# Pairwise field projection on one core: the next x by a gather on GpSimd without eight partitions, and its transpose eight steps later

## What is computed

```
xi = x[:, pi, :]                              # 2048 x 496 x 64
xj = x[:, pj, :]
proj = einsum('bpd,pod->bpo', xi, W)          # each row of xi by its pair's matrix
return proj * xj                              # 2048 x 496 x 64, 260 MB
```

## Time and profile before

| | |
|---|---|
| median of three runs | 684.69 us |
| the profiled execution | 684.55 us |
| its span | 682.7 us |
| PE busy | 573.4 us (84%) |
| DVE busy | 409.3 us (60%) |
| POOL busy | 391.9 us (57%) |
| ACT busy | 208.4 us (31%) |
| bytes moved by DMA | 285.20 MB, 418 GB/s over the span |
| of the chain that ended last: matmuls (line 294) | 47% |
| of it: DMA x_sb<-x_dram | 37% |

### The profile page before, as it was taken

How to read it: one execution, slowest core, us unless ns; L and a number is a source line. 1 busy time by engine, 2 the same in 40 slices (tenths; PEclk the granted TensorE clock), 3 DMA queues, 4 the chain that set the end, 5 groups by cost and what they waited for, 6 DMA issues and landing times.

```text
span 682.7 us, 7003 instructions
## 1 busy us (share of the span) xinstructions
PE 573.4 (84%) x2704; PEld 363.3 (53%) x2704; DVE 409.3 (60%) x528; ACT 208.4 (31%) x257; POOL 391.9 (57%) x228
## 2 busy tenths in 40 slices
PE   6899989979799796988969889697996979979930
PEld 4565646546465564645646456464654646546520
DVE  1677775837567473764837638386583756837730
ACT  3334333323233333332323323233332323332300
POOL 1768674646566374674646836468464665647720
PEclk9999999989899898998989989899898989989975
DMA  8999999999999999999999999999999999999995
GB/s 336 386 426 425 439 438 423 434 436 428 432 432 431 432 428 436 435 427 428 431 427 429 428 404 410 428 421 407 426 426 424 422 415 429 399 439 419 421 421 233
DMA packets 15648, 285.20 MB, mean 418 GB/s; under 512 B 1744, under 2 KB 1872, under 8 KB 3856
## 3 DMA queue, kind: packets, MB, share of 16 engines
q1 hardware_dynamic: 13472, 270.28, 93.3%
q10 hardware_dynamic: 2160, 14.75, 5.1%
HBM read 24.97 MB, written 260.05 MB: 417 GB/s over the span
## 4 chain that ended last, share of the span: by engine, by line
PE 55%; DMA 37%; DVE 2%; SPq 1%; issue 1%; ACT 0%; DVEq 0%; ACTq 0%
PE proj L294 47%; DMA x_sb<-x_dram 37%; PE proj L272 7%; DVE staged L338 2%; SPq L199 1%; ACT staged L260 0%; SPq L203 0%; SPq L197 0%; SPq L196 0%; SPq L195 0%; DVEq L133 0%; ACTq L259 0%
## 5 line engine op out<-in xcount | busy, mean ns | idle before, releaser
L338 DVE TENSOR_TENSOR staged<-proj,x_sb 128x1024 f32<-128x1024 f32 (+7 forms) x528 | 409.3, 826 | 246.5 <-PE proj L294 210.8
L221 POOL TENSOR_TENSOR staged<-staged,x_sb 128x1024 f32<-128x1024 f32 (+4 forms) x224 | 391.7, 1755 | 261.4 <-ACT staged L260 258.4
L294 PE MATMUL proj<-w_sb,x_t 64*128 64x512 f32 (+7 forms) x2432 | 518.7, 533 | 3.6 <-DVE staged L338 2.1
L294 PEld LDWEIGHTS proj<-w_sb,x_t 64*128 64x128 f32 x2432 | 313.1, 188 | 204.3 <-issue 121.6
L260 ACT ACTIVATE staged<-proj 128x1024 f32<-128x1024 f32 (+4 forms) x224 | 174.6, 787 | 356.5 <-PE proj L294 329.1
L272 PE MATMUL proj<-ident_sb,x_sb 128*128 128x128 f32 x256 | 52.6, 390 | 71.2 <-DMA x_sb<-x_dram 71.2
L272 PEld LDWEIGHTS proj<-ident_sb,x_sb 128*128 128x128 f32 x256 | 47.1, 208 | 80.3 <-DMA x_sb<-x_dram 79.8
L236 ACT ACTIVATE x_t<-proj 128x1024 f32<-128x1024 f32 x32 | 32.5, 1024 | 86.2 <-PE proj L272 86.1
L311 PE MATMUL proj<-ident_sb 128*128 128x128 f32 x16 | 3.4, 405 | 5.6 <-DMA ident_sb<-ident_dram 5.6
L311 PEld LDWEIGHTS proj<-ident_sb 128*128 128x128 f32 x16 | 3.2, 223 | 5.6 <-DMA ident_sb<-ident_dram 5.6
L236 ACT ACT_TABLE_LOAD x1 | 1.3, 1283 | 1.2 <-PEq L368 1.2
## 6 DMA issues: line engine op xcount, KB each, us to landing
out_dram<-staged SPq DMA_DIRECT2D x14, 4896.0 KB, 26.0
out_dram<-staged SPq DMA_DIRECT2D x14, 3936.0 KB, 23.0
out_dram<-staged SPq DMA_DIRECT2D x14, 3776.0 KB, 27.7
out_dram<-staged SPq DMA_DIRECT2D x14, 3264.0 KB, 27.7
x_sb<-x_dram ACTq DMA_DIRECT2D x14, 1024.0 KB, 17.8
out_dram<-staged SPq DMA_DIRECT2D x2, 1952.0 KB, 16.8
out_dram<-staged SPq DMA_DIRECT2D x2, 1824.0 KB, 20.6
out_dram<-staged SPq DMA_DIRECT2D x2, 1728.0 KB, 21.8
```

Source lines behind the costliest of these rows:

```text
L221: last = nc.gpsimd.tensor_tensor(product, product, x_sb[tile.parity][:, j * dim:(j + n) * dim], ALU.mult)
L294: last = nc.tensor.matmul(proj[b][h][:, at:at + width], x_t[tile.parity][half, i // 2, :], w_sb[half, col:col + width], start=True, stop=True)
L338: last = nc.vector.tensor_tensor(staged_part(item, i, j, n), proj[b][h][:, at:at + n * dim], x_sb[tile.parity][:, j * dim:(j + n) * dim], ...
```

## The change

Three things change. The turn moves from before step 10 to before step 18, on PE and on ACT. The next x is fetched by POOL instead of ACT, before POOL's step 4: an indirect DMA that takes for partition p the row of x named in `rows_sb[p, tile]`. For partitions 28 to 35 that table holds a number beyond x, and the bounds check leaves them out. These eight partitions (64 KB) are loaded by ACT with a plain DMA, where it loaded all of x before. POOL waits for that small load before it issues the gather; PE waits for both at the turn. The table of row numbers (128 x 16 numbers, 8 KB) is loaded once by SP ahead of the first store, and the second tile's x gets a semaphore of its own.

```diff
-TURN_BEFORE = 10
+TURN_BEFORE = 18
 LOAD_BEFORE = 3
+GATHER_BEFORE = 4
...
+SKIPPED = range(28, 36)
+NO_ROW = 1 << 20
...
-            sp.dma_start(x_sb[1][:], x[P:2 * P, :]).then_inc(x_loaded[1], 16)
+            sp.dma_start(x_sb[1][:], x[P:2 * P, :]).then_inc(x_second_loaded, 16)
+            sp.dma_start(rows_sb[:], rows).then_inc(rows_loaded, 16)
...
         @block.gpsimd
         def _(pool):
+            def load_x(tile):
+
+                _, b, use = list(items(Tile(tile.number - 1, 1 - tile.parity, None)))[-1]
+
+                pool.wait_ge(emptied[b][1], use + 1)
+                pool.wait_ge(pool_scaled[group_of[pool_steps[-1]]], tile.number)
+                to = tile.number + 1
+
+                pool.wait_ge(x_rest_loaded[1 - tile.parity], 16 * (to // 2))
+                nc.gpsimd.indirect_dma_start(
+                    x_sb[1 - tile.parity][:], None, x,
+                    bass.IndirectOffsetOnAxis(ap=rows_sb[:, to:to + 1], axis=0),
+                    bounds_check=batch - 1, oob_is_err=False).then_inc(x_loaded[1 - tile.parity], 16)
+
             def emit(tile):
                 for item, b, use in items(tile):
+                    if item == GATHER_BEFORE and not tile.first and not tile.last:
+                        if tile.number == 1:
+                            pool.wait_ge(rows_loaded, 16)
+                        load_x(tile)
...
-                act.dma_start(x_sb[1 - tile.parity][:], x[bass.ds((tile.number + 1) * P, P), :]
-                              ).then_inc(x_loaded[1 - tile.parity], 16)
+                row = (tile.number + 1) * P
+                act.dma_start(x_sb[1 - tile.parity][SKIPPED.start:SKIPPED.stop, :],
+                              x[row + SKIPPED.start:row + SKIPPED.stop, :]
+                              ).then_inc(x_rest_loaded[1 - tile.parity], 16)
...
                     if item == "turn":
-                        pe.wait_ge(x_loaded[1 - tile.parity], 16 * tile.half + 16)
+
+                        if tile.first:
+                            pe.wait_ge(x_second_loaded, 16)
+                        else:
+                            loads = tile.half + 1 if tile.parity else tile.half
+                            pe.wait_ge(x_loaded[1 - tile.parity], 16 * loads)
+                            pe.wait_ge(x_rest_loaded[1 - tile.parity], 16 * loads)
...
+    rows = np.arange(batch, dtype=np.uint32).reshape(-1, P).T.copy()
+    rows[SKIPPED.start:SKIPPED.stop] = NO_ROW
```

More of the change, by code:

```diff
@@ L6 @@
 F32 = mybir.dt.float32
+U32 = mybir.dt.uint32
 ALU = mybir.AluOpType
@@ L71, in __init__, with field_pair_project @@
         self.first = isinstance(number, int) and number == 0
-def field_pair_project(nc, x, w, ident, out, fields, dim):
+def field_pair_project(nc, x, w, ident, rows, out, fields, dim):
     batch = x.shape[0]
@@ L145, in field_pair_project @@
         ident_sb = sb("ident_sb", [P, P])
+        rows_sb = sb("rows_sb", [P, tiles], U32)
         staged = [sb(f"staged{k}", [P, n * dim]) for k, (_, n) in enumerate(slot_range)]
@@ L151, in field_pair_project @@
         ident_loaded = sem("ident_loaded")
+        rows_loaded = sem("rows_loaded")
         x_first_loaded = [sem(f"x_first_loaded{h}") for h in range(2)]
+        x_second_loaded = sem("x_second_loaded")
         x_loaded = [sem(f"x_loaded{h}") for h in range(2)]
+        x_rest_loaded = [sem(f"x_rest_loaded{h}") for h in range(2)]
         w_loaded = [sem(f"w_loaded{c}") for c in range(len(w_cuts) - 1)]
@@ L237, in turned_out, with load_skipped @@
                         "p k b -> p (k b)"), proj[b][h][:], ACT.Copy).then_inc(emptied[b][h], 1)
-            def load_x(tile):
+            def load_skipped(tile):
                 _, b, use = list(items(Tile(tile.number - 1, 1 - tile.parity, None)))[-1]
@@ L250, in emit @@
                     if item == LOAD_BEFORE and not tile.first and not tile.last:
-                        load_x(tile)
+                        load_skipped(tile)
                     if item == "turn":
@@ L366 @@
         "ident_dram": np.eye(P, dtype=np.float32),
+        "rows_dram": rows,
     }
@@ L369 @@
                    dynamic_dma_scratch_size=DMA_SCRATCH)
-    aps = [nc.dram_tensor(n, a.shape, F32, kind="ExternalInput").ap() for n, a in arrays.items()]
+    aps = [nc.dram_tensor(n, a.shape, U32 if a.dtype == np.uint32 else F32, kind="ExternalInput").ap()
+           for n, a in arrays.items()]
     out = nc.dram_tensor("out_dram", (batch, pairs * dim), F32, kind="ExternalOutput").ap()
```

## The result

The changed kernel took 689.92 us (689.72 to 690.12, 4 runs), the kernel before 684.64 us; the ratio is 1.0077, 95% interval 1.0065 to 1.0090. It is slower by 5.3 us. The forecast was 673.5 us; the time lies above the range.

What follows compares the result with a forecast made beforehand. One of 16 DMA engines, slower by 1.02 us a tile, was the bound; its relieved end at 669.5, plus 2.85 after it, 1 for gathered rows and 0.3 for the table, made 673.6, stated as 673.5 us; range 668 to 686 us.

Steps and rivals of the forecast that it cites:

- The reading of the bound: DMA engines: one of 16 is slower by 1.02 us a tile and binds; PE's 5.1 us wait for x is slack.
- The turn alone: Turn before step 18 on PE and ACT: removes the 5.1 us wait for x, but alone is worth 0.
- The gather at GpSimd: Gather on POOL: its issue costs 1.5 us, POOL stays at 31 us a tile, under 40, so cost 0.
- GpSimd's wait for the small load: POOL before the gather: 5 us for ACT's 64 KB load, covered by POOL's spare time, cost 0.
- rival C: POOL becomes the bound if the small load takes 17.8 us: 42.6 us a tile, 706 us; chance 0.04.
- The extra microsecond for gathered rows: Gathered rows may cost more than plain ones, 0 to 10 us in all; 1 us added to the forecast.
- the central term: Eight partitions less in the gather: slow engine at 5 rows, 0.91 us a tile less, 12.7 us in 14 gathers.
- rival B: Slow engine gets a ninth row from ACT's small load: +4.2 us, 688.8 us; with dearer gathered rows, together 0.14.
- the forecast's own split: Rows of x per engine: two engines lose four each, and ACT's eight rows go to eight engines, one each.
- The size of the forecast's own case: Slow engine at five rows, engines with nine ending about the same, near 669.5 us: 673.5 us; chance 0.60.

Runs made afterwards that it cites:

- run 1: The kernel before with only the turn moved from before step 10 to before step 18: 684.63 us, ratio 0.9998.
- run 2: The changed kernel with no partition left out of the gather and no small load by ACT: 684.65 us, ratio 0.9998.
- run 10: The changed kernel with only partitions 16 to 19 left out, loaded by a plain GpSimd DMA before its step 3, none by ACT: 684.81 us, ratio 1.0000.
- run 5: The changed kernel with only partitions 16 to 19 left out of the gather and loaded by ACT: 679.31 us, ratio 0.9921.
- run 6: The changed kernel with only partitions 12 to 15 left out of the gather and loaded by ACT: 684.79 us, ratio 1.0001.
- run 9: The changed kernel with partitions 16 to 19 and 48 to 51 left out, loaded by ACT in two four-row DMAs: 684.05 us, ratio 0.9994.
- run 4: The changed kernel with partitions 12 to 19 left out in place of 28 to 35: 678.82 us, ratio 0.9904.
- run 11: As run 10, but with GpSimd's four-row load before step 1 instead of step 3: 678.96 us, ratio 0.9912.
- run 12: As run 5, but with partitions 16 to 19 left out and loaded by ACT only in every other tile: 678.42 us, ratio 0.9910.
- run 3: The changed kernel with partitions 4 to 11 left out in place of 28 to 35: 689.08 us, ratio 1.0062.
- run 8: The changed kernel with partitions 28 to 35 loaded by ACT in two DMAs of four rows instead of one of eight: 685.6 us, ratio 1.0026.
- run 7: As run 4, but with the turn back before step 10: 789.64 us, ratio 1.153.

## Why the prediction was wrong

**What held.** The reading of the bound: one of 16 DMA engines slower than the rest, PE's wait for x being slack (run 1: the wait gone, 684.63 us). The turn alone at 0 (run 1). The gather at GpSimd at 0 (run 2: 684.65 us; 1.04 us of issue where I took 1.5). GpSimd's wait for the small load, covered: it isn't the bound, rival C didn't come, though such a load takes about 8 us (8.22 us in run 10) where I took 5. The extra microsecond for gathered rows wasn't needed.

**The step that failed** is the central term, "If the slow engine is among those that lose rows". I took 8 - 4 + 1 = 5 rows of x for it. It serves partitions 16 to 19 (runs 5 and 6) and 48 to 51 (the packets of run 9), loses none of 28 to 35 and gets one of ACT's eight: 9 rows, as its packets show. The split itself, two engines with five rows and six with nine, was right; the slow engine stood on its wrong side. Nine rows on it is rival B, which I priced at 688.8 us and gave, with its like, 0.14. Nothing in the trace had spoken for 28 to 35; I let a case that the profile could not tell from others carry 0.60, when two engines of 16 lose rows and eight get one. Counted by engines alone, on the forecast's own split, 2 in 16 are relieved, 6 in 16 get a ninth row and 8 in 16 keep eight; that count was open to me and gives B more than the forecast.

**The size of B.** 4.2 us were forecast for it, 5.3 measured, or 0.38 us a row (5.28 / 14) in place of 0.303; in the whole tiles it is 41.40 - 41.08 = 0.32. Rows added to other engines come out dearer, about 0.5 us (run 9).

**The size of the forecast's own case.** Run 4 is that case: the slow engine has five rows, six engines have nine. It took 678.8 us, not 673.5. So the forecast would have been some 5 us too low even with the slow engine where I put it. The engines left at the end are about as many as have nine rows of x (six in run 4, four in runs 5 and 11), which speaks for added rows that cost more than the 0.303 us of the sum, by which nine-row engines were to need 40.35 us a tile. It isn't shown: run 12 halved the added rows and gained nothing clear. Where the rest goes is open; the runs add the row always with a small DMA of its own, and nothing was tried that adds the one without the other.

**Whose rows.** By the runs alone: leaving out 16 to 19 helps, 12 to 15, 4 to 11 and 28 to 35 don't; an eight-row load by ACT puts a row on the slow engine, a four-row one doesn't. The Trainium skill (DMA: Bandwidth & Descriptors, The descriptor swizzle) puts 16 to 19 on engine 4, 12 to 15 on 3, 28 to 31 on 7 and 32 to 35 on 0. Together with the same page's rule (Why a DMA increments its semaphore by 16 and not by 1) by which an eight-row transfer from ACT uses the eight lowest engines and a four-row one the four lowest, a slow engine 4 gives nine rows in the changed kernel and in run 3 (689.9 and 689.1 us), eight in runs 6 and 8 (684.8 and 685.6), five in run 4 (678.8) and four in run 5 (679.3). More rows go with more time, down to eight; five and four can't be told apart. The packets give the same counts, so the runs agree with both. They don't agree with the remark of the same page of the Trainium skill (Latency and other measured facts) that engines 7 and 15 are usually the slow ones; by its map it is engine 4 here, which the forecast had nothing to tell from the others.

## What to carry to other kernels

A transfer over 128 partitions lands when the slowest DMA engine's rows have; look behind all computing for a stretch in which the share is one sixteenth, and find out whose partitions they are (leave out four at a time) before rebalancing. Skipping the right four partitions in a gather gave 0.9% here, the wrong eight cost 0.8% with the same code. A small load that takes over the skipped rows adds rows to the same few engines each time, so count rows for every engine, the slow one too; and a wait of 5 us a tile on the chain may be worth nothing while another resource is full.

## What was not expected of the hardware

- One engine in 16 needs 41.07 us for what the others do in about 40.05 (an estimate from 432 GB/s), with a kernel that loads and stores the same bytes on all: its store packets of 26 and 31 KB take some 33 ns more each. It was the engine of partitions 16 to 19 on three chips: run 4 ran on one, run 9 on another, runs 5 and 11 on a third.
- One row of 8 KB more per tile on each of four engines, which move 40 rows of 8 to 39 KB in that time, cost nearly the whole gain: 684.05 us with ten rows of x on them (run 9), 679.3 with nine (run 5). The packet of such a row takes 0.309 us.
- A wait of some 8 us a tile that was free with the late turn cost 105 us with the early one (run 7).
